# Gated cross-attention and quantised FFN: order of the last batch's softmax, Pool's passes and the context matrix in the attention stage

## The chip, the cores and the metric

One core of one Trainium2 chip runs the kernel as a single launch. The metric is the device time in microseconds (us). The kernel before takes 461.97 us, the median of 3 runs (461.82 to 462.2).

## The reference

Four batches of 1024 tokens of width 256 attend to 154 context rows each, then go through an FFN with fake quantisation. Cut to what matters here:

```python
h = layernorm(x)                                   # per batch, 1024 x 256
Sim = (h @ w1)[:, None] + (ctx @ w2)[None, :] + (h * w3) @ ctx.T + b
hq = softmax(Sim, axis=ctx) @ ctx                  # 1024 x 256
Batt = softmax(max(Sim, axis=ctx), axis=tokens)    # 1024 weights per batch
hc = Batt @ h                                      # one row of 256 per batch
x1 = x + tanh(g0) * (concat[h, hq, h*hq, h*hc] @ W_qv + b_qv)
y = layernorm(x1)
out = x1 + tanh(g1) * ffn(y)                       # 768 hidden, quantised weights and activations
```

`hc` needs the maxima of a whole batch, so `h*hc @ W` is folded into a batch matrix: `h @ (W[0] + hc * W[3])`. That matrix `we` can be made only when all 1024 tokens of the batch have scores.

## The kernel before, in words

The kernel has an attention stage, which makes `x1` and `y` (the first 196 us of the profile), and a quantised FFN stage behind it. The change touches only the attention stage. Its 4096 tokens are cut into N = 16 units of 256 tokens, four to a batch (NP = 4). The work is written as a hand-made software pipeline: each engine has its own loop over slots m = 0, 1, 2, ..., 22, with b = m // 4 and s = m % 4, and in a slot each engine issues, in the order of its own loop, pieces of work for different units. Semaphores alone tie the engines to each other, and each engine executes strictly in the order written. Unit n gets its layernorm and its transpose in slot n, its scores in slot n+1, its attention in slots n+2 and n+3, and its projection, residual and second layernorm from slot n+7 on (LAG = 7). Batches 0 to 2 have their end in a slot in which the next batch is already under way; the last batch (b = 3) has nothing behind it.

What each engine does, with the names that the text uses:

- **TensorE (PE)**, L691 to L727. `project(n)` is 12 matmuls, 24 records in the trace (L576, L578, L582): the third part, L582, multiplies by `we` and in the first unit of a batch waits for it (`we_rdy`, L580). In slots 7, 11 and 15 the first unit of a batch is cut into `project_first` (L601, L603) early in the slot and `project_rest` (L613) at its end, which waits for `we`; the last batch's first unit, unit 12, is not cut: it is `project(12)` in slot 19. `turn_h`, `turn_a`, `turn_y` are transposes, `score(n)` L545, `attend(n)` L564, `turn_w` L676 transposes the FFN's weights. `batch_max(b)` (L641) spreads the batch's minimum over the partitions, `batch_cols(b)` (L648, L649) sums the weighted rows into `hc`. In slot 17 `batch_max(3)`, and in slot 18 `batch_cols(3)`, stand in front of `project`, so all later work of TensorE waits behind them.
- **ScalarE (ACT)**, L942 to L975. `exps(n)` L865, `normed(n)` L874, `turned_*` and `attended(n)` copy out of PSUM, `batch_exp(b)` (L921) makes the 1024 token weights, `row_weigh(b)` (L927) applies half of them, `weight_f(i)` (L932) converts a weight matrix.
- **VectorE (DVE)**, L1328 to L1385. `scored(n)` (L1143), `stats(n)`, `residual(n)` (L1167 to L1178: residual, then mean and deviation), `norm_x1(n)` (L1184, two instructions, makes `yb` out of `xa`), `max_y(n)` (L1224), `attended(n)` (L1159), `batch_max(b)` (L1230, L1232), `batch_shift(b)` (L1236), `summary(b)` (L1240 to L1248, makes `we`), `weight_scales`, `weight_unit`, `weight_values(i)` (L1288), `weight_part` (L1294).
- **GpSimd (POOL)**, L448 to L476. `y_std(n)` (L392) is a tiny power that turns the variance of `residual(n)` into the deviation for which `norm_x1(n)` waits; `row_std` (L388) is the same for the first layernorm. The long passes are `row_weigh(b)` (L418, four instructions), `row_pair(b)` (L425), `row_add(b)` (L431, L433, L435), `bias_x(n)` (L443), `weight_q(i, half)` (L405) and `weight_n(i)` (L411).

The chain from the last score of a batch to its `we` runs: DVE `scored`, DVE `batch_max`, PE `batch_max`, DVE `batch_shift`, ACT `batch_exp`, ACT and POOL `row_weigh`, POOL `row_pair` and `row_add`, PE `batch_cols`, DVE `summary`. For the last batch the order of before spreads it over slots 16 to 18. SyncE's queue loads inputs and stores `x1` and the output; it has no part in the change.

The waits that carry most of the argument are these:

```python
# PE, L645: batch_cols waits for POOL's last addition
pe.wait_ge(hs_rdy, b + 1)
# PE, L579: the matrix of the batch, in its first unit
if s == 0:
    pe.wait_ge(we_rdy, b + 1)
# DVE, L1181: norm_x1 waits for POOL's deviation
dve.wait_ge(rstd2_rdy, n + 1)
```

Of the kernel before, what the change touches and what calls it, by code (L numbers as in the profile page):

```python
# [39 lines left out]
B, S, D = 4, 1024, 256  # L40
# [26 lines left out]
def build(nc, x, ctx, g_xattn, g_ffn, w_sim, b_sim, w_qv, b_qv, w_gate, w_up, w_down, out):  # L67
# [145 lines left out]
    with ExitStack() as stack:  # L213
# [70 lines left out]
        N = B * NP  # L284
        W_AT = [10, 14, 17]
        SCALES_AT = [9, 13, 15]
        VALUES_AT = [12, 16, 18]
        NORMS_AT = [12, 18, 19]
        NF = 2 * NP
        WARM = 24  # L290
        HC = P + D
# [89 lines left out]
        def _(pool):  # L381
# [31 lines left out]
            def row_weigh(b):  # L413

                par = b % 2
                pool.wait_ge(eb_rdy, b + 1)
                for t in range(TB // 2, TB):
                    i_ = pool.tensor_scalar(h[:, par, t, :], h[:, par, t, :], eb[:, t:t + 1], 1.0, ALU.mult, ALU.mult)  # L418
                i_.then_inc(hp_rdy, 1)
# [28 lines left out]
            for m in range(N + LAG):  # L448
                b, s = m // NP, m % NP
                if s == 3 and 4 <= m < N + 4:  # L450
                    for n in range(2):
                        bias_x(m - 5 + n)
                if s == 1 and 1 <= b <= B:
                    row_weigh(b - 1)
                if m == N:
                    for n in range(2):
                        bias_x(m - 4 + n)
                if m == N + 1:
                    row_pair(b - 1)
                    row_add(b - 1)  # L460
                if LAG <= m < L + LAG:
                    y_std(m - LAG)
                if s == 1 and 1 <= b < B:
                    row_pair(b - 1)
                if s == 2 and 1 <= b < B:
                    row_add(b - 1)
                if 1 <= m and m + 3 < N:
                    row_std(m + 3)
                if s == 0 and 4 <= m < N:
                    for n in range(2):  # L470
                        bias_x(m - 4 + n)
                for i in range(3):
                    if m in (SCALES_AT[i] + 1, SCALES_AT[i] + 2):
                        weight_q(i, m - SCALES_AT[i] - 1)
                    if m == NORMS_AT[i]:
                        weight_n(i)  # L476
            y_std_last()

# [27 lines left out]
        def _(pe):  # L506
# [184 lines left out]
            for m in range(N + LAG):  # L691
                b, s = m // NP, m % NP
                late = s == 3 and b < B
                if m == N:
                    score(m - 1)
                if m == N + 1:
                    batch_max(b - 1)
                if m == N + 2:
                    batch_cols(b - 1)
                if LAG <= m and not late:  # L700
                    project(m - LAG, b - 1 if s == 1 and b < B else None)
                if LAG <= m and late:
                    project_first(b - 1)
                if m < N:
                    turn_h(m)
                if s == 3 and b + 1 < B:
                    turn_context(b + 1)
                if 1 <= m < N:
                    score(m - 1)
                if 2 <= m <= N + 1:  # L710
                    turn_a(m - 2)
                if s == 1 and b == 1:
                    batch_max(b - 1)
                if s == 3 and 1 <= b < B:
                    batch_cols(b - 1)
                if 3 <= m <= N + 2:
                    attend(m - 3)
                if LAG < m:
                    turn_y(m - LAG - 1)
                if s == 3 and b + 1 < B:  # L720
                    context_bias(b + 1)
                if LAG <= m and late:
                    project_rest(b - 1)
                if m in W_AT:
                    weight_max(W_AT.index(m))
                for i in TURN_AT.get(m, ()):
                    turn_w(i)  # L727
# [106 lines left out]
        def _(act):  # L834
# [107 lines left out]
            for m in range(N + LAG):  # L942
                b, s = m // NP, m % NP
                if m < N:
                    turned_h(m)
                if s == 3 and b + 1 < B:
                    turned_context(b + 1)
                if s == 1 and 1 < b <= B:
                    batch_exp(b - 1)
                if m == N + 1:  # L950
                    row_weigh(b - 1)
                if NF <= m + 1 < N and s < 3:
                    norm_x(m + 1)
                if 2 <= m <= N + 1:
                    turned_a(m - 2)
                if 1 <= m <= N:
                    exps(m - 1)
                if NF <= m + 1 < N and s == 3:
                    norm_x(m + 1)
                if 3 <= m <= N + 2:  # L960
                    attended(m - 3)
                if 1 <= m <= N:
                    normed(m - 1)
                if s == 1 and b == 1:
                    batch_exp(b - 1)
                if s == 1 and 1 <= b < B:
                    row_weigh(b - 1)
                if LAG < m:
                    turned_y(m - LAG - 1)
                if s == 3 and b + 1 < B:  # L970
                    context_k(b + 1)
                if m in VALUES_AT:
                    weight_f(VALUES_AT.index(m))
                for i in TURN_AT.get(m, ()):
                    turned_w(i)  # L975
# [116 lines left out]
        def _(dve):  # L1092
# [235 lines left out]
            for m in range(N + LAG - 1):  # L1328
                b, s = m // NP, m % NP
                late = s == 3 and b < B  # L1330
                if m == N + 1:
                    batch_shift(b - 1)
                if 4 <= m <= N + 3:
                    attended(m - 4)
                if m == N:
                    scored(m - 1)
                    batch_max(b - 1)
                    normed(m - 1)
                if m == N + 2:
                    summary(b - 1)  # L1340
                if m == 0:
                    norm_x(3)
                if 3 <= m and m + 1 < NF:
# [7 lines left out]
                if s == 0 and LAG < m <= N:  # L1351
                    norm_x1(m - LAG - 1)
                    max_y(m - LAG - 1)
                if LAG <= m and not late:
                    residual(m - LAG)
                if 1 <= m < N:
                    scored(m - 1)
                if s == 0 and 1 <= b < B:
                    batch_max(b - 1)
                if 1 <= m and m + 3 < N:  # L1360
                    if s == 1:
                        dve.wait_ge(xr_in[b], 16)
                    stats(m + 3)
# [3 lines left out]
                    batch_shift(b - 1)  # L1367
                if LAG <= m and not late:
                    norm_x1(m - LAG)
                if s == 3 and 1 <= b < B:  # L1370
                    summary(b - 1)
                if LAG <= m and not late:
                    max_y(m - LAG)
                for i in range(3):
                    if m == SCALES_AT[i]:
                        weight_scales(i)
                    if m == W_AT[i]:
                        weight_unit(i)
                    if m == VALUES_AT[i]:
                        weight_values(i)  # L1380
                if LAG <= m and late:
                    residual(m - LAG)
# [237 lines left out]
```

## Time and profile before

| what | value |
|---|---|
| median of 3 runs | 461.97 us (461.82 to 462.2) |
| the profiled execution's own time | 459.6 us |
| its span in the trace | 457.8 us |
| mean granted TensorE clock | 0.992 of full |
| TensorE matmul, busy | 433.4 us, 95% of the span |
| VectorE, busy | 363.4 us, 79% |
| ScalarE, busy | 274.6 us, 60% |
| GpSimd, busy | 110.7 us, 24% |
| attention stage | the first 196 us of the span |
| FFN stage | from 196 us to the end |

All times of the trace are counted from the start of the span. In a timeline row the columns are: start, length, engine, line and operation, what is written and read, how many such instructions stand in a row, and in brackets how long the engine had been idle before, and which engine and line ended that. Slot borders can be read from TensorE: slot 11 ends with the matmuls of L613 at 86.81, slot 15 with those at 126.15, and slot 18 starts with L648 at 152.54. The profiled execution was 2.4 us quicker than the median of the runs, and its time is 1.8 us above its span.

### The profile page before, as it was taken

The page shows a single profiled execution, that of the slowest core. Times are in us where ns is not written, and L with a number is a line of the kernel's source. Part 1 is how long each engine was busy: PE and PEld are TensorE (multiplying, and loading weights), DVE is VectorE, ACT ScalarE, POOL GpSimd, SP SyncE. Part 2 cuts the span into 40 slices and gives each one's busy share as a digit, 9 for nine tenths or more (in the row PEclk, how much of TensorE's full clock was granted, in tenths as well). Part 3 has the DMA queues.
Part 4 walks back from the last instruction along what each step waited for, and adds up shares of the span by engine and source line. Part 5 has one row for each costly group of instructions (what it writes and reads, how often), then busy time and mean ns, then how long its engine had stood idle before and what let it go on. Part 6 is the DMA issues. An engine that isn't in the chain of part 4 may idle for free.

```text
span 457.8 us, 6771 instructions
## 1 busy us (share of the span) xinstructions
PE 433.4 (95%) x2432; PEld 297.2 (65%) x2432; DVE 363.4 (79%) x652; ACT 274.6 (60%) x346; POOL 110.7 (24%) x109
## 2 busy tenths in 40 slices
PE   4899999999997698999999999999999999999997
PEld 3788898889876586744444444444444444788886
DVE  6786789797777488886433789999998889898874
ACT  2677365556525023284334599999296779987760
POOL 1239274365744453100000013334100000000000
PEclk9999999999999799999999999999999999999999
DMA  7950002000200020110000000000000000344442
GB/s 242 314 166 0 1 2 92 1 0 3 92 1 0 0 94 0 43 50 0 0 0 0 1 1 1 0 0 0 1 0 0 0 0 0 117 139 139 137 137 70
DMA packets 20672, 21.13 MB, mean 46 GB/s; under 512 B 825, under 2 KB 20392, under 8 KB 20648
## 3 DMA queue, kind: packets, MB, share of 16 engines
q1 hardware_dynamic: 20628, 20.82, 14.4%
q8 instruction: 14, 0.23, 0.2%
q14 instruction: 10, 0.08, 0.1%
q10 hardware_dynamic: 20, 0.00, 0.0%
HBM read 12.43 MB, written 8.39 MB: 45 GB/s over the span
## 4 chain that ended last, share of the span: by engine, by line
PE 44%; DVE 24%; issue 19%; ACT 7%; POOL 4%; DMA 1%; ACTq 0%; POOLq 0%; DVEq 0%
PE ps L785 12%; PE ps L750 9%; PE ps L755 5%; DVE cols L1452 4%; DVE yb L1184 4%; PE ps L576 3%; PE ps L578 3%; PE ps L582 3%; DVE hid L1468 2%; ACT hid L1012 2%; PE ps L564 2%; PE ps L545 1%; PE ps L613 1%; POOL h L418 1%; ACT ag L1017 1%
## 5 line engine op out<-in xcount | busy, mean ns | idle before, releaser
L750 PE MATMUL ps<-xh,wuh 128*128 128x512 f16 x192 | 72.8, 379 | 0.8 <-DVE gq L1491 0.8
L750 PE MATMUL ps<-xh,wul 128*128 128x512 f16 x192 | 72.8, 379 | 0.0
L755 PE MATMUL ps<-xl,wuh 128*128 128x512 f16 x192 | 57.2, 379 | 0.0
L1431 DVE TENSOR_REDUCE cols<-hid x10 | 22.9, 2286 | 24.3 <-ACT hid L989 24.3
L785 PE MATMUL ps<-wdl,oh 128*128 128x256 f16 x168 | 37.4, 273 | 0.0
L785 PE MATMUL ps<-wdh,oh 128*128 128x256 f16 x168 | 37.4, 273 | 0.0
L750 PE MATMUL ps<-xh,wgl 128*128 128x512 f16 x96 | 36.4, 379 | 0.0
L750 PE MATMUL ps<-xh,wgh 128*128 128x512 f16 x96 | 36.4, 379 | 0.0
L989 ACT ACTIVATE hid<-ps 128x2048 f32 x10 | 18.8, 1875 | 27.5 <-PE ps L755 27.5
L750 PEld LDWEIGHTS ps<-xh,wuh 128*128 (+1 forms) x192 | 18.8, 98 | 24.0 <-issue 1.8
L482 POOL PARTITION_ALL_REDUCE cols<-cols x4 | 1.5, 374 | 135.0 <-DVE cols L1391 135.0
L755 PEld LDWEIGHTS ps<-xl,wuh 128*128 (+1 forms) x192 | 18.8, 98 | 22.7
L750 PEld LDWEIGHTS ps<-xh,wul 128*128 (+1 forms) x192 | 18.8, 98 | 22.4
L1184 DVE TENSOR_SCALAR yb<-xa,cols 128x256 f32<-128x256 f32 x30 | 23.7, 832 | 11.6 <-POOL cols L392 11.6
L564 PE MATMUL ps<-aT,cx 77*128 77x256 f32 x128 | 30.5, 381 | 0.0
L857 ACT ACTIVATE hT<-ps 128x512 f32<-128x512 f32 x16 | 9.4, 590 | 33.9 <-PE ps L531 33.9
L1491 DVE TENSOR_TENSOR gq<-gq,ps 128x2048 bf16<-128x2048 int16 x11 | 25.1, 2286 | 5.3 <-ACT au L1041 5.3
L1074 ACT ACTIVATE oq<-hid,cols 128x1536 int16 (+1 forms) x15 | 23.6, 1571 | 9.6 <-DVE ol L1547 9.6
L1468 DVE CUSTOM_DVE_ANT_0 hid<-ag,sq 128x2048 f32<-128x2048 int16 x12 | 29.1, 2424 | 0.2
L755 PE MATMUL ps<-xl,wgh 128*128 128x512 f16 x96 | 28.6, 379 | 0.1
L1452 DVE TENSOR_REDUCE cols<-ps 128x1 f32<-128x2048 f32 x12 | 27.4, 2286 | 1.6 <-PE ps L755 1.6
L576 PE MATMUL ps<-wv,hqT 128*128 128x256 f32 x104 | 27.7, 391 | 0.0
(223 smaller groups left out, 1039.8 us busy)
## 6 DMA issues: line engine op xcount, KB each, us to landing
x_scratch<-xa SPq DMA_DIRECT2D x4, 1024.0 KB, 4.4
xo<-x_scratch SPq DMA_DIRECT2D x16, 256.0 KB, 2.7
out_dram<-xo SPq DMA_DIRECT2D x15, 256.0 KB, 2.2
xa<-in_x SPq DMA_DIRECT2D x3, 1024.0 KB, 12.7
xa<-in_x SPq DMA_DIRECT2D x4, 256.0 KB, 4.5
wv<-in_L_xattn_W_qv SPq DMA_DIRECT2D x1, 1024.0 KB, 8.4
wr<-in_L_ffn_w_gate SPq DMA_DIRECT2D x1, 768.0 KB, 10.1
wr<-in_L_ffn_w_up SPq DMA_DIRECT2D x1, 768.0 KB, 11.5
```

The lines of the kernel that those rows point to most:

```text
L564: mm = pe.matmul(hq_bank[:, d * PT:(d + 1) * PT], cx[b][0:JP, k, d * P:(d + 1) * P], aT[0:JP, n % 3, k, :], start=k == 0, stop=k == 1)
L576: pe.matmul(o_, hqT[:, par, d, q], wv[:, KD + d, :], start=d == 0, stop=False)
L750: pe.matmul(ps[hf][:, q, :], w_[:, d, ds(k * P, P)], xh[:, d, n], start=d == 0 and w_ is wh, stop=False)
L755: mm = pe.matmul(ps[hf][:, q, :], wh[:, d, ds(k * P, P)], xl[:, d, n], start=False, stop=d == KD - 1)
L785: mm = pe.matmul(down_ps(par)[:, t], o_[:, par, k, q], w_[:, k, :], start=not low and k == 0 and w_ is wdh, stop=low and k == KF - 1)
L989: act.activation(unit(hid, k, hf), ps_half(hf), ACT.Copy).then_inc(half_free[hf], 1)
L1074: act.activation(oq[:, par], hid[:, :, ds(c * CD, CD)], ACT.Copy, scale=c_co).then_inc(oqa_rdy, 1)
L1184: i_ = dve.tensor_scalar(yb[:, n % 2, t, :], xa[:, 2 * n + t, :], mv2[:, t, 0:1], rstd2[:, t:t + 1], ALU.subtract, ALU.mult)
L1431: dve.tensor_reduce(gmx[:, ds(k * 2 + hf, 1)], unit(hid, k, hf), AX.X, ALU.max, apply_absolute_value=True).then_inc(gm_done, 1)
L1452: dve.tensor_reduce(umx[:, u:u + 1], ps_half(u % 2), AX.X, ALU.max, apply_absolute_value=True).then_inc(half_free[u % 2], 1)
L1468: dve.tensor_tensor_reduce(half_of(hid, u), ag[:, u % 2, :], sq[u % 2][:], 1.0, 0.0, ALU.mult, ALU.max, pmx[:, u:u + 1]).then_inc(p_rdy, 1)
L1491: dve.tensor_tensor(g_.bitcast(BF16), g_, ps_half(hf), ALU.mult).then_inc(half_free[hf], 1)
```

## The change

It moves work within the slots of the four hand-written orders; no instruction is added or removed.

- POOL: `bias_x` of slots 8 and 12 (and 4) moves from the end of the slot to its head, in front of `y_std` and `row_std`. `row_pair(b-1)` follows `row_weigh(b-1)` directly, in front of `y_std`. For the last batch both move from slot 17 to slot 16, and `row_add(3)` stays in slot 17, in front of `y_std(10)`. `weight_n(1)` moves in slot 18 in front of `y_std(11)`; `weight_n(2)` moves from the end of slot 19 to slot 20 in front of `y_std(13)`.
- PE: `batch_max(3)` moves from the head of slot 17 into slot 16 behind `turn_a(14)`; `batch_cols(3)` stays in slot 18 but moves behind `project(11)`.
- ACT: in slot 16 `exps(15)` goes ahead of `turned_a(14)`, and `batch_exp(3)` and `row_weigh(3)` come from slot 17 into slot 16.
- DVE: `batch_shift(3)` comes from the head of slot 17 into slot 16, with `normed(15)` directly ahead of it, both behind `norm_x1(8)` and `max_y(8)` and in front of `residual(9)`. `summary(3)` stays in slot 18 and moves behind `residual(11)`. `weight_values(2)` moves in slot 18 from the end to in front of `residual(11)`. `summary(1)` and `summary(2)`, in slots 11 and 15, move in front of `stats` and `normed`.

```diff
-        NORMS_AT = [12, 18, 19]
+        NORMS_AT = [12, 18, 20]
...
# POOL
-                if s == 1 and 1 <= b <= B:
-                    row_weigh(b - 1)
-                if m == N:
+                if s == 0 and 4 <= m < N + 4:
                     for n in range(2):
                         bias_x(m - 4 + n)
+                if s == 1 and 1 <= b < B or m == N:
+                    row_weigh(b - 1)
+                    row_pair(b - 1)
                 if m == N + 1:
-                    row_pair(b - 1)
                     row_add(b - 1)
+                for i in range(3):
+                    if m == NORMS_AT[i] and i > 0:
+                        weight_n(i)
                 if LAG <= m < L + LAG:
                     y_std(m - LAG)
-                if s == 1 and 1 <= b < B:
-                    row_pair(b - 1)
...
-                if s == 0 and 4 <= m < N:
-                    for n in range(2):
-                        bias_x(m - 4 + n)
...
-                    if m == NORMS_AT[i]:
+                    if m == NORMS_AT[i] and i == 0:
                         weight_n(i)
# PE
-                if m == N + 1:
-                    batch_max(b - 1)
-                if m == N + 2:
-                    batch_cols(b - 1)
...
-                if s == 1 and b == 1:
+                if s == 1 and b == 1 or m == N:
                     batch_max(b - 1)
+                if m == N + 2:
+                    batch_cols(b - 1)
# ACT
-                if s == 1 and 1 < b <= B:
+                if s == 1 and 1 < b < B:
                     batch_exp(b - 1)
-                if m == N + 1:
-                    row_weigh(b - 1)
+                if m == N:
+                    exps(m - 1)
...
-                if 1 <= m <= N:
+                if m == N:
+                    batch_exp(b - 1)
+                if 1 <= m < N:
                     exps(m - 1)
...
-                if s == 1 and 1 <= b < B:
+                if s == 1 and 1 <= b < B or m == N:
                     row_weigh(b - 1)
# DVE
-                if m == N + 1:
-                    batch_shift(b - 1)
...
-                    normed(m - 1)
-                if m == N + 2:
-                    summary(b - 1)
+                if m == VALUES_AT[2]:
+                    weight_values(2)
...
+                if m == N:
+                    normed(m - 1)
+                    batch_shift(b - 1)
                 if LAG <= m and not late:
                     residual(m - LAG)
+                if m == N + 2:
+                    summary(b - 1)
...
+                if s == 3 and 2 <= b < B:
+                    summary(b - 1)
...
-                if s == 3 and 1 <= b < B:
+                if s == 3 and b == 1:
                     summary(b - 1)
...
-                    if m == VALUES_AT[i]:
+                    if m == VALUES_AT[i] and i < 2:
                         weight_values(i)
```

## Rows read from the trace of the kernel before

**Rows 1.** The page: busy time, share of the span, instructions of each engine.

```profile
PE 433.4 (95%) x2432; PEld 297.2 (65%) x2432; DVE 363.4 (79%) x652; ACT 274.6 (60%) x346; POOL 110.7 (24%) x109
```

**Rows 2.** Busy time by stretch, the second half of the attention stage (then clock, DMA).

```profile
126.00:196.00 70.00, 60.63 (x309) 51.16 (x310) 52.20 (x115) 19.06 (x39) 27.57 (x26) 0.95 0.09 30
```

**Rows 3.** Timeline of TensorE, slots 11, 15 and 18 to 21.

```profile
85.98 0.76 PE L522 MATMUL ps<-cxT,w2b 128*128 128x154 f32 x4 [0.98 <-DVE cols L1242]
86.81 1.99 PE L613 MATMUL ps<-we,hT 128*128 128x256 f32 x8
...
126.15 2.00 PE L613 MATMUL ps<-we,hT 128*128 128x256 f32 x8 [0.86 <-DVE we L1248]
...
152.54 1.01 PE L648 MATMUL ps<-ones,h 128*128 128x1 f32 x4 [6.49 <-POOL h L435]
...
153.84 2.05 PE L576 MATMUL ps<-wv,hqT 128*128 128x256 f32 x4
...
160.68 1.89 PE L564 MATMUL ps<-aT,cx 77*128 77x256 f32 x8
...
162.84 1.03 PE L576 MATMUL ps<-wv,hqT 128*128 128x256 f32 x4
...
168.02 0.60 PE L621 MATMUL ps<-ident,yb 128*128 128x128 f32 x4
...
176.36 0.66 PE L621 MATMUL ps<-ident,yb 128*128 128x128 f32 x4 [1.25 <-DVE yb L1184]
...
179.43 1.03 PE L576 MATMUL ps<-wv,hqT 128*128 128x256 f32 x4
```

**Rows 4.** Busy time by microsecond around the stall; the third column from the right is PEclk.

```profile
150.00:151.00 1.00, 0.00 (x0) 0.00 (x0) 0.00 (x0) 0.00 (x0) 0.92 (x2) 0.60 0.00 0
...
156.00:157.00 1.00, 1.00 (x4) 0.73 (x4) 0.88 (x5) 0.00 (x0) 0.00 (x0) 0.50 0.00 0
157.00:158.00 1.00, 1.00 (x6) 0.90 (x5) 0.93 (x4) 0.00 (x0) 0.00 (x0) 0.98 0.00 0
```

**Rows 5.** Timeline of GpSimd, slots 17 to 19.

```profile
145.95 1.84 POOL L418 TENSOR_SCALAR h<-h,cols 128x256 f32<-128x256 f32 x4 [3.96 <-ACT cols L921]
...
151.76 0.72 POOL L435 TENSOR_TENSOR h<-h 128x256 f32<-128x256 f32 x1
...
153.11 1.48 POOL L405 TENSOR_TENSOR wr<-wr,wri 128x768 f32<-128x768 f32 x1
...
163.63 2.77 POOL L411 TENSOR_TENSOR wr<-wr,wsc 128x1536 f32<-128x1536 f32 x1
166.37 2.60 POOL L443 TENSOR_TENSOR xa<-xa,txb 128x512 f32<-128x512 f32 x2
```

**Rows 6.** Timeline of VectorE in slot 18: the two instructions of norm_x1(11), one by one.

```profile
163.71 2.85 DVE L1184 TENSOR_SCALAR yb<-xa,cols 128x256 f32<-128x256 f32 x1 [0.81 <-POOL cols L392]
...
166.48 1.35 DVE L1184 TENSOR_SCALAR yb<-xa,cols 128x256 f32<-128x256 f32 x1
```

**Rows 7.** Timeline of VectorE, slots 15 to 19.

```profile
125.22 0.88 DVE L1248 SCALAR_TENSOR_TENSOR we<-wv,cols 128x256 f32<-128x256 f32 x2
...
132.09 1.38 DVE L1232 TENSOR_SCALAR diag<-ident,cols 128x128 f32<-128x128 f32 x1
...
140.57 1.88 DVE L1184 TENSOR_SCALAR yb<-xa,cols 128x256 f32<-128x256 f32 x2 [0.81 <-POOL cols L392]
...
153.18 1.88 DVE L1184 TENSOR_SCALAR yb<-xa,cols 128x256 f32<-128x256 f32 x2 [6.28 <-POOL cols L392]
...
157.81 0.88 DVE L1248 SCALAR_TENSOR_TENSOR we<-wv,cols 128x256 f32<-128x256 f32 x2
...
173.13 3.18 DVE L1184 TENSOR_SCALAR yb<-xa,cols 128x256 f32<-128x256 f32 x2 [0.81 <-POOL cols L392]
```

**Rows 8.** Timeline of ScalarE in slot 17: the last batch's exponentials.

```profile
145.47 0.28 ACT L921 ACTIVATE cols<-cols 128x8 f32<-128x8 f32 x1
```

**Rows 9.** Timeline of GpSimd and of TensorE in slots 4 to 6.

```profile
28.59 2.78 POOL L443 TENSOR_TENSOR xa<-xa,txb 128x512 f32<-128x512 f32 x2
...
34.12 0.66 PE L554 MATMUL ps<-ident,sc 128*77 128x128 f32 x4 [0.68 <-ACT sc L874]
```

## The prediction

> **What bounds the kernel now.** I read the page first: TensorE is busy for 95% of the span [rows 1], so a gain can only be idle or slow time of TensorE. Busy time by stretch says where that is: of the 70 us from 126 to 196 us TensorE works 60.6, at a mean clock of 0.95 [rows 2]. Next I read TensorE's timeline there, for its gaps and for who ended each [rows 3]. The largest is 6.49 us in front of 152.54: `batch_cols(3)` waits for Pool's last addition (151.76 + 0.72 [rows 5]), and `project(11)` stands behind it. The clock falls during this gap: it is 0.60 in the microsecond from 150 to 151, stays at 0.50 (1.2 of 2.4 GHz) until 157, and is back after it [rows 4]. So `project(11)` took 6.84 us (153.84 to 160.68) where `project(12)` took 5.18 (162.84 to 168.02) [rows 3], 1.66 lost. `batch_cols` took 1.30 (152.54 to 153.84); if half of that is the clock, 0.65 is lost too. Stall and clock together: 6.49 + 1.66 + 0.65 = 8.8 us. Smaller gaps are 0.98 in slot 11, 0.86 in slot 15 and 1.25 in front of 176.36 [rows 3].
>
> Then I read the chain behind the large gap. Batch_exp(3) runs at 145.47 [rows 8], since it is in slot 17 behind `weight_f(1)`; Pool weighs the rows from 145.95 on and ends at 152.48 [rows 5]. Vector waits 6.28 us for `y_std(10)` behind that same Pool work, until 153.18 [rows 7].
>
> **Slots 11 and 15.** `summary` goes ahead of `stats` (slot 11) and of `normed` (slot 15). In slot 11 it saves the 1.15 us of `stats`; the matmuls at 86.81 can start when `we` is there, at about 85.7, and the 0.98 wait of the row before goes too: 1.1 us. In slot 15 `normed` waits for exponentials and holds `summary` back; ahead of it, `we` is ready at 124.95 in place of 126.1 (its end by 125.22 + 0.88 [rows 7]), and TensorE starts the matmuls of 126.15 at about 125.2: 1.0 us. What `stats` and `normed` give up, 1.3 us, is covered, as their users come a slot later.
>
> **Slots 16 and 17**, on the clock of before (slot 11's gain taken off at the end). TensorE runs `score(15)`, `project(9)` and `turn_a(14)` until 133.7, `batch_max(3)` until 133.9, `attend(13)` until 135.6. Vector: `diag` is held by `weight_q` until 132.4. Now `bias_x(12)` and (13), 1.25 each (2.60 for two [rows 5]), hold the two halves of `norm_x1(8)` until 133.7 and 134.95; `max_y(8)`, `normed(15)`, `batch_shift(3)` end at 136.1. Batch_exp(3) ends at 136.6, before at 145.9 [rows 8]: 9.3 sooner. Pool's `row_weigh` (1.84 [rows 5]) and `row_pair` (1.3) end at 139.8, `y_std(9)` at 140.5, `weight_q` (1.48 [rows 5]) at 142.0, the three additions of `row_add(3)` (3.3, and 0.8 for a Vector instruction let in between) at 146.1. TensorE reaches `batch_cols(3)` at 149.3, behind `project(10)` and `project(11)`. So **the stall of 6.49 and the half clock behind it are gone**, with 3 us to spare. Every moved instruction of POOL is in this; none issues a DMA, and SyncE's queue isn't touched.
>
> **What is late next.** Vector. Norm_x1(9) has to wait until 140.5 for `y_std(9)`, which now stands behind `row_weigh` and `row_pair`, and is then held by `weight_q` and the first addition until 143.4. `max_y`, `weight_values(1)`, `attended(13)` and `residual(10)` follow: 148.7. Then y_std(10) at 149.45, `weight_q` (1.48) until 150.95 and, directly behind, `weight_n(1)` (2.77) until 153.75 [rows 5]: the two halves of `norm_x1(10)` end at 151.1 and 153.9. TensorE has finished `attend(15)` at 151.5 and wants that `yb`: **first new wait, 2.4 us**. Vector goes on with `max_y`, `weight_unit(2)`, `attended(14)`, `weight_values(2)`, 3.3 us, to 157.2; `residual(11)`, 1.9, to 159.1; `summary(3)`, 1.26 (0.15 + 0.22 + 0.88 [rows 7]), to 160.35. The diff puts the last two in this order. Before, `we` was there at 158.7 (157.81 + 0.88 [rows 7]), long ahead of its use. Now `project(12)` starts at 154.4 and at 156.1 wants `we`: **second new wait, 4.2 us**. It resumes at 160.35 and ends at 163.8, before at 168.02 [rows 3].
>
> After that: norm_x1(11) is held by `bias_x(14)` and (15) only, not by `weight_n(1)`: 2.1 us in place of 4.13. `weight_n(2)` is still the next pass of Pool after `y_std(12)`, with nothing between; here the diff changes nothing, and norm_x1(12) keeps its 3.18 us [rows 7]. Its `yb` is there at 169.95 and TensorE wants it at 170.8, so the 1.25 goes. Turning the weights in slot 20 waits about 0.4 for Vector's `weight_part`. `project(14)` starts at 172.9, before at 179.43 [rows 3]: 6.5 us sooner. Check by waits: pure work between 125.2 and `project(14)` is 40.7 us, so of before's 53.3 us from 126.15, 12.6 were waits and half clock; now they are 2.4 + 4.2 + 0.4 = 7.0. 12.6 - 7.0 + 1.0 (slot 15) = 6.6, the same within 0.1. From 180 us on nothing changes its order, and the FFN stage needs only the last unit: the gain is kept whole.
>
> **Slots 4 to 13.** In slot 4 the two `bias_x` leave 28.59, where they held a Vector layernorm for 2 us and so TensorE for 0.68 at 34.12 [rows 9] and 0.44 before. At 23.3 they hold `attended(0)` and norm_x(5) instead; `normed(3)` comes 1.4 later and TensorE waits 1.05 for `turn_a(3)`. I get 1.05 lost and 1.25 won, 0.2 us gained; bounds are 1.0 lost (nothing comes back) and 1.2 gained. In slots 8 to 13 the moved passes run where Pool was idle, and `row_pair` ahead of `y_std` changes 1.3 us of blocking into 1.3 us of waiting: nothing, as TensorE has work queued for over 2 us there; if that cover is gone, 0.6 per slot.
>
> **The sum.** 6.5 (slots 15 to 21) + 1.1 (slot 11) + 0.2 = 7.8 us: 459.6 becomes 451.8 for the profiled execution. The median of the runs is 2.4 us above it, so 461.97 becomes 454.2.
>
> **The rivals.**
> - *Vector is less late than worked out* (0.17). The new waits are 7 us because Pool's passes catch `norm_x1(10)` twice. If its second half gets in ahead of `weight_n(1)`, the first wait goes and the second shrinks to about 3. Against: [rows 6]. Gain 9.5 to 11, 451 to 452.5.
> - *A queue of Pool passes keeps Vector out until it is empty* (0.07). Then norm_x1(9) also waits for all three additions, 2.3 us more down to `summary(3)`: gain 5.5, 456.5. Against: two separate ends in [rows 6]. The Trainium skill, "SBUF — State Buffer", section "SBUF: two separate sides", says that whichever of the two engines starts first holds the shared ports "for the whole instruction" while the other "fully blocks"; it doesn't say who wins at the border, and by its strictest reading this rival holds.
> - *The clock falls in the new waits* (0.18). Before, it fell within the idle stretch of 6.49 us [rows 3, 4]; the second new wait is two thirds as long, with only 2 us of work between it and the first. Half clock behind it costs about what it cost before, 2.3: gain 5.5, 456.5. For: the waits stand close together. Against: no shorter wait here (up to 1.25 us) moved the clock. The Trainium skill, "TensorE: Matmul & The Clock Gate", Part 1, says that the array drops to half clock when idle and regains full clock only by sustained activity; this speaks against the change, for it makes one long wait into two nearer ones.
> - *Slower* (0.04). The same clock, but it stays down: after the first new wait TensorE's work never runs long enough to bring it back before the next wait. From 7.8 us of work run at half rate on, the change loses: between 154 us and the end of the stage TensorE has some 35 us of work. If 12 us of it run at half rate, 466. Against: before, 4.7 us after work had resumed the clock was back [rows 4].
> - *No change* (0.02): another wait of the same length takes the place of 152.54, which would need `hs_rdy` at 155, 9 us later than I get.
> - The rest, 0.52, is the forecast, with a range of its own of 452.7 to 455.5.
>
> **How the numbers follow.** Range 451.0 to 457.8: it takes in the first three rivals and the bounds of slot 4, and leaves out a combination of losses. A measurement of this kernel can tell about 0.2% (0.9 us) from no change. Faster 0.93, same 0.03, slower 0.04.
>
> **What would show it.** Right: no gap over 0.5 us in front of L648; batch_exp(3) near 135.5 on the new clock; `project(12)` with a gap in front of its first L582 of 3 to 4 us, ended by DVE L1248; a gap near 2 us in front of `turn_y(10)`; PEclk 1.00 around it; `project(14)` near 171.6. Wrong: a gap in front of L648 still ended by POOL L435, an L582 without a wait, a clock of 0.5 near 158, or FFN rows whose lengths differ from before.

## The result, and the profile after

The changed kernel takes 456.42 us, the median of 4 runs (454.66 to 457.08), against 462.09 for the kernel before. One of the 4 runs of before took 760.31 us, far from the other three (461.82 to 462.20), and only those three count in the ratio. The ratio is 0.9883 with a 95% interval of 0.9836 to 0.9930: faster, by 1.2%, which is 5.4 us (5.7 by the two medians). Two more sets of runs gave 0.9882 (0.9852 to 0.9912) and 0.9872 (0.9850 to 0.9895). The forecast was 454.2 with a range of 451.0 to 457.8, so the time lies inside the range, but 2.2 us above the number, where two of the rivals stood (456.5: the clock falls in the new waits, or a queue of Pool passes keeps Vector out); the traces decide between them below. The profiled execution took 455.91 us, where 451.8 was forecast for it; it is 3.7 us under the profiled one of before (459.6), which was a quick one of its kind.

TensorE's timeline after, slots 11, 15 and 18 to 22; a project(n) begins with L574 here, where it was L576 before (answers to [rows 3]):

```profile
85.00 0.77 PE L520 MATMUL ps<-cxT,w2b 128*128 128x154 f32 x4 [0.17 <-DVE cols L1240]
85.82 1.99 PE L611 MATMUL ps<-we,hT 128*128 128x256 f32 x8
...
124.34 1.99 PE L611 MATMUL ps<-we,hT 128*128 128x256 f32 x8
...
148.46 0.50 PE L646 MATMUL ps<-ones,h 128*128 128x1 f32 x4
...
152.80 0.66 PE L619 MATMUL ps<-ident,yb 128*128 128x128 f32 x4 [1.78 <-DVE yb L1182]
...
160.25 2.07 PE L580 MATMUL ps<-we,hT 128*128 128x256 f32 x4 [5.06 <-DVE we L1246]
...
166.03 0.60 PE L619 MATMUL ps<-ident,yb 128*128 128x128 f32 x4
...
175.37 1.03 PE L574 MATMUL ps<-wv,hqT 128*128 128x256 f32 x4
```

The stall of 6.49 us in front of `batch_cols(3)` is gone: L646 starts at 148.46 with nothing to wait for. In its place stand the two waits that were forecast: 1.78 us for the `yb` of norm_x1(10), and 5.06 us for the batch matrix in the middle of `project(12)`. The 16 matmul records behind the second took 5.78 us (160.25 to 166.03) where 3.45 is their time at full clock (164.57 to 168.02 in the trace of before). The clock says why (answers to [rows 4]; the third column from the right is PEclk):

```profile
154.00:156.00 2.00, 1.19 (x6) 0.71 (x4) 1.93 (x6) 0.09 (x1) 0.00 (x0) 1.00 0.00 0
156.00:158.00 2.00, 0.00 (x0) 0.00 (x0) 1.89 (x7) 1.48 (x1) 0.00 (x0) 0.99 0.19 68
158.00:160.00 2.00, 0.00 (x0) 0.00 (x0) 1.94 (x3) 0.00 (x0) 2.00 (x3) 0.50 1.02 347
160.00:163.00 3.00, 2.75 (x7) 2.21 (x8) 2.97 (x5) 0.00 (x0) 1.32 (x1) 0.50 0.25 82
```

It falls near 158, inside the second wait, is at 0.61 in the microsecond from 164 and at full behind it. That is a loss of 5.78 - 3.45 = 2.33 us.

The other side of the waits is Vector, which from 146 to 162 us has hardly a gap left. Its timeline after (answers to [rows 6, 7]) and Pool's (answers to [rows 5]):

```profile
148.41 4.34 DVE L1182 TENSOR_SCALAR yb<-xa,cols 128x256 f32<-128x256 f32 x2 [0.81 <-POOL cols L392]
...
155.91 0.75 DVE L1165 SCALAR_TENSOR_TENSOR xa<-ps,cols,xa 128x512 f32<-128x512 f32 x1
...
157.83 0.16 DVE L1238 RECIPROCAL cols<-ps 128x1 f32<-128x1 f32 x1
158.03 0.22 DVE L1240 TENSOR_SCALAR cols<-ps,cols 128x2 f32<-128x2 f32 x1
158.28 1.91 DVE L1246 SCALAR_TENSOR_TENSOR we<-wv,cols 128x256 f32<-128x256 f32 x2
160.12 1.67 DVE L1182 TENSOR_SCALAR yb<-xa,cols 128x256 f32<-128x256 f32 x2
```

```profile
148.34 1.48 POOL L405 TENSOR_TENSOR wr<-wr,wri 128x768 f32<-128x768 f32 x1
149.78 2.82 POOL L411 TENSOR_TENSOR wr<-wr,wsc 128x1536 f32<-128x1536 f32 x1
158.00 0.69 POOL L392 TENSOR_TENSOR cols<-cols 128x2 f32<-128x2 f32 x1 [5.41 <-DVE cols L1176]
158.66 2.67 POOL L443 TENSOR_TENSOR xa<-xa,txb 128x512 f32<-128x512 f32 x2
```

Norm_x1(10) takes 4.34 us for 0.7 us of work: `weight_q` and `weight_n(1)` run back to back on Pool in front of it. And the last two instructions of `summary(3)`, 0.88 us before [rows 7], take 1.91: `bias_x` starts at 158.66, directly behind `y_std(11)`, and holds the second of them.

### The profile page after: what moved, and what is told of

Its sections match the earlier page's. It is cut to its first block, busy times and chain, and to the rows that moved or that the text cites. A ratio compares the mean times of both kernels' runs of the same rounds, so it can differ in the third digit from the quotient of the medians.

```text
span 454.1 us, 6771 instructions
## 1 busy us (share of the span) xinstructions
PE 433.1 (95%) x2432; PEld 297.5 (66%) x2432; DVE 363.0 (80%) x652; ACT 275.0 (61%) x346; POOL 110.9 (24%) x109
## 4 chain that ended last, share of the span: by engine, by line
PE 42%; DVE 26%; issue 20%; ACT 6%; POOL 4%; DMA 1%; ACTq 0%; POOLq 0%; DVEq 0%
PE ps L781 12%; PE ps L746 9%; PE ps L751 5%; DVE cols L1454 4%; DVE yb L1182 4%; PE ps L580 3%; PE ps L574 2%; PE ps L576 2%; DVE hid L1470 2%; ACT hid L1010 2%; PE ps L543 2%; PE ps L562 2%; POOL h L418 1%; ACT ag L1015 1%; DVE st L1169 1%
## 5 line engine op out<-in xcount | busy, mean ns | idle before, releaser
L580 PE MATMUL ps<-we,hT 128*128 128x256 f32 x104 | 27.7, 390 | 5.1 <-DVE we L1246 5.1
L1182 DVE TENSOR_SCALAR yb<-xa,cols 128x256 f32<-128x256 f32 x30 | 24.7, 865 | 8.6 <-POOL cols L392 8.6
```

The source lines that it names most:

```text
L580: mm = pe.matmul(o_, hT[:, par, d, q], we[:, par, d, :], start=False, stop=d == KD - 1)
L1182: i_ = dve.tensor_scalar(yb[:, n % 2, t, :], xa[:, 2 * n + t, :], mv2[:, t, 0:1], rstd2[:, t:t + 1], ALU.subtract, ALU.mult)
```

## The experiments

The base of each comparison is the kernel before, run on the same chip beside it. Line numbers of the versions differ by a few from those of the changed kernel. Where a gain over the changed kernel is given, its median on the same chip is taken: 455.66 us for experiments 2, 3 (the first version) and 4, and 455.84 for the others. The traces don't all start alike: over the profiles of experiments 1 to 6 `batch_cols(3)` begins between 148.27 and 149.26 us, so a difference of times under 1 us between two of them says little unless that start is the same.

**1. The changed kernel again**, as a base, in two sets.

> The changed kernel once more, as the base of the other three. Theory A (the changed kernel loses 5.1 us in project(12)'s wait for the batch matrix and 2.4 us to the half clock behind it; Vector's order makes the wait): 456 us, 5.5 to 6.5 us under the kernel before, a wait of 5 us in front of the first L580 of project(12), the clock at half from about 158 to 164 us. Theory B (the moment of the clock's fall is chance): runs of the same kernel differ by 1 to 3 us, and a profile with the clock at full behind the wait turns up.

> The changed kernel again, as the base for the three others on the same chip: 456 us, 1.2% under the kernel before.

Measured 455.66 us in the first set and 455.84 in the second. What theory B asked for turned up in part: single runs of the kernel lie between 454.6 and 457.4, and the clock in the first set's profile behaves otherwise than in the one above:

```profile
153.00:154.00 1.00, 1.00 (x6) 0.88 (x5) 0.90 (x5) 0.56 (x1) 0.00 (x0) 0.58 0.00 0
154.00:155.00 1.00, 1.00 (x4) 0.77 (x3) 0.97 (x4) 0.04 (x1) 0.00 (x0) 0.50 0.00 0
...
156.00:157.00 1.00, 0.77 (x2) 0.10 (x1) 0.97 (x3) 1.00 (x1) 0.00 (x0) 0.71 0.00 0
157.00:158.00 1.00, 0.00 (x0) 0.00 (x0) 0.90 (x7) 0.40 (x1) 0.11 (x1) 1.00 0.51 173
...
160.00:161.00 1.00, 0.86 (x2) 0.77 (x3) 1.00 (x2) 0.00 (x0) 1.00 (x1) 0.50 0.58 190
```

Here it falls behind the first wait already, is full again at 157, and is at half once more when the second wait ends; `project(12)` ends at 165.29. The profile of the second set is like the one above (5.07 us of wait, `project(12)` ends at 165.86). So the moment of the fall differs between executions of one kernel, but all three pay behind the second wait. A profile with the clock at full there did not turn up.

**2. Summary(3) in front of residual(11).** It asks whether the place of the wait matters, or only Vector's total lateness.

```diff
-                if LAG <= m and not late:
-                    residual(m - LAG)
                 if m == N + 2:
                     summary(b - 1)
+                if LAG <= m and not late:
+                    residual(m - LAG)
```

> The changed kernel with summary(3) in front of residual(11) instead of behind it in slot 18. Theory A: summary follows weight_values(2) at 155.9 us and isn't held by bias_x, so the matrix is there at 157.2 in place of 160.2; the second wait falls from 5.1 to 2 us and the clock stays at full; but then turn_y(11) waits some 2 us for a norm_x1(11) that comes behind it, and project(14) starts 2.5 us sooner than in the changed kernel: 453.5 us. Theory C (the wait is only where Vector's lateness shows; its place does not matter): project(14) starts at the same time as in the changed kernel, 456 us, with the wait in front of turn_y(11).

Measured 453.50 us, ratio 0.9835 (0.9803 to 0.9867). TensorE's and Vector's timelines of this version:

```profile
157.50 1.58 PE L580 MATMUL ps<-we,hT 128*128 128x256 f32 x4 [2.11 <-DVE we L1246]
...
162.86 0.66 PE L619 MATMUL ps<-ident,yb 128*128 128x128 f32 x4
```

```profile
156.56 0.88 DVE L1246 SCALAR_TENSOR_TENSOR we<-wv,cols 128x256 f32<-128x256 f32 x2
...
160.18 2.62 DVE L1182 TENSOR_SCALAR yb<-xa,cols 128x256 f32<-128x256 f32 x2 [0.81 <-POOL cols L392]
```

The matrix takes 0.88 us, not 1.91, and the wait is 2.11. Theory A's time came out, partly by luck; its working did not in one part: the clock fell here too, after 158, and the half rate hid the wait that was foreseen in front of turn_y(11), as its `yb` comes at 162.8 anyway. Theory C, 456 us, falls.

**3. TensorE kept busy in the wait**: 20 matmuls whose results nobody reads.

```diff
                     if s == 0:
+                        if b == B - 1:
+                            for i in range(20):
+                                pe.matmul(hT_bank[:, 0:P], ones[:], ident[:], start=True, stop=True)
                         pe.wait_ge(we_rdy, b + 1)
```

> The changed kernel with 20 matmuls of 128x128 (float32, results unused) into a free bank between the second and the third part of project(12), in front of its wait for the batch matrix: some 4.4 us of work in a wait of 5.1. Theory A: the wait keeps its end (160.2 us), the clock stays at full, project(12) ends 2.3 us sooner (163.7 in place of 166.0) and all behind it too: 453.7 us. Theory C (Vector would be late anyway, so the clock costs nothing): project(12) is shorter but residual(12) starts no sooner, 456 us.

Measured 458.62 us, slower than the changed kernel, through a flaw of the edit: it stands in a loop over both halves of `project(12)`, so a second 20 (4.4 us) ran behind the wait. Against the kernel before the ratio is 0.9939 (0.9920 to 0.9958). With these 4.4 us taken off it would be some 454, but that is arithmetic, no measurement. The same with `and t == 0`:

> The changed kernel with the 20 matmuls once, between the second and third part of the first half of project(12) (in r_warm they stood in both halves, and the second 20 lay on the path: 4.4 us). Theory A: the wait for the batch matrix still ends at 160.2 us, the clock is at full there, project(12) is through 2.0 to 2.3 us sooner than with half clock behind the wait, and since Vector's residual(12) waits for it all behind comes sooner: 453.7 us against 455.7. Theory C (Vector would be late anyway): 455.7 us, no gain.

Measured 454.59 us, ratio 0.9844 (0.9812 to 0.9877) against 0.9882 and 0.9872 for the changed kernel; the intervals overlap, so this alone decides nothing. In its profile the clock had fallen already behind the first wait, the 20 matmuls ran at half rate for part of their way and ended at 161.05, 0.9 us after the matrix was there. So both waits were filled, with 7 and 18 matmuls:

> The changed kernel with 7 such matmuls (1.5 us) in the wait of turn_y(10) and 18 (4.0 us) in the wait for the batch matrix, since the clock was seen to fall in the first wait already. Theory A: the clock stays at full all through, project(12) ends at 163.6 us in place of 165.3 to 166, and the time is 1.7 to 2.3 us under the changed kernel, with less spread between runs. Theory C (Vector would be late anyway): the same time as the changed kernel.

Measured 453.55 us (453.21 to 454.13 in 5 runs), ratio 0.9814 (0.9798 to 0.9829) against 0.9872 (0.9850 to 0.9895) for the changed kernel beside it. Its clock and TensorE's timeline (L583 is the third part of project(12), L622 turn_y(11)):

```profile
158.00:160.00 2.00, 1.18 (x11) 0.98 (x9) 1.97 (x3) 0.00 (x0) 2.00 (x3) 1.00 1.04 346
160.00:162.00 2.00, 1.77 (x8) 1.59 (x9) 1.97 (x4) 0.00 (x0) 1.29 (x1) 1.00 0.33 109
```

```profile
160.23 1.13 PE L583 MATMUL ps<-we,hT 128*128 128x256 f32 x4 [1.05 <-DVE we L1252]
...
163.78 0.60 PE L622 MATMUL ps<-ident,yb 128*128 128x128 f32 x4
```

The matrix comes no sooner (160.2 us, as in the changed kernel; `batch_cols(3)` begins at 148.44 here and at 148.46 there), the clock is at full, and project(12) is through at 163.78 in place of 166.03 (165.29 and 165.86 in the other two profiles): 2.25 us. The medians differ by 2.3. So **the half clock behind the new wait costs the changed kernel 2.3 us**, and nothing else covers it; theory C falls. The runs spread over 0.9 us (5 runs) where those of the changed kernel beside them spread over 1.9 (4 runs). That the clock makes the whole of that difference isn't shown: the slowest of the 4, 457.4 us, has the highest mean clock of them, 0.993.

**4. Weight_n(1) back behind y_std(11).** It tests the rule for Pool's passes by itself.

```diff
                 for i in range(3):
-                    if m == NORMS_AT[i] and i > 0:
+                    if m == NORMS_AT[i] and i > 1:
                         weight_n(i)
...
-                    if m == NORMS_AT[i] and i == 0:
+                    if m == NORMS_AT[i] and i < 2:
                         weight_n(i)
```

> The changed kernel with weight_n(1) back behind y_std(11), at the end of slot 18. Theory A (a Vector instruction waits out each Pool pass under way, one gets in at each border): norm_x1(10) takes 1.9 us in place of 4.3, the 1.8 us wait of turn_y(10) goes, Vector reaches summary(3) 2.4 us sooner, but now weight_n(1) holds its second half until 159: the matrix is there at about 159.2, one wait of 6.2 us in place of 1.8 and 5.1, the clock falls: 455.3 us. Theory D (where a pass stands does not matter as long as it is off TensorE's path): same time as the changed kernel, 456.2 us, within 0.5.

Measured 455.15 us, ratio 0.9864 (0.9831 to 0.9896). By the time alone theories A (455.3) and D (within 0.5 of 456.2) can't be told apart, and against the changed kernel's 455.66 nothing is gained clear of the spread; by the trace they can. Vector and Pool of this version:

```profile
148.55 1.88 DVE L1182 TENSOR_SCALAR yb<-xa,cols 128x256 f32<-128x256 f32 x2 [0.82 <-POOL cols L392]
...
155.97 3.42 DVE L1246 SCALAR_TENSOR_TENSOR we<-wv,cols 128x256 f32<-128x256 f32 x2
```

```profile
156.34 2.77 POOL L411 TENSOR_TENSOR wr<-wr,wsc 128x1536 f32<-128x1536 f32 x1
159.07 2.71 POOL L443 TENSOR_TENSOR xa<-xa,txb 128x512 f32<-128x512 f32 x2
```

Norm_x1(10) takes 1.88 us, as worked out, and the second half of the matrix waits out `weight_n(1)` until 159.4 (expected 159.2). TensorE has one wait of 6.12 us in front of 159.45 (expected 6.2). The place of the pass decides which Vector instruction it falls on: `weight_n(1)` holds `norm_x1(10)` in the changed kernel and `summary(3)` here. That the time stays nearly the same is no sign that the place doesn't matter: one wait went (1.78 us), the other grew (5.06 to 6.12), and more of TensorE's time behind it passes at half clock (6.0 us, until about 165.4, in place of 4.5, until about 164.8).

**5. Pool waits for norm_x1 before its next pass.**

```diff
                 pool.tensor_tensor(rstd2, vp2, mhalf[:, 0:2], ALU.pow).then_inc(rstd2_rdy, 1)
+                if 9 <= n <= 12:
+                    pool.wait_ge(y_rdy, n + 1)
```

> The changed kernel in which Pool, behind y_std(9) to y_std(12), waits until norm_x1 of the same unit is done before it starts its next long pass. Theory A (what makes Vector late is that a pass of Pool starts in front of norm_x1 each time): norm_x1(9), (10), (12) take 0.7 us each in place of 2.8, 4.3 and 3.2, the passes fall on weight_values and attended instead, the matrix is there at 156.4 in place of 160.2, the wait of turn_y(10) is gone: 449.5 us with the clock at full, 451 to 451.5 with it at half behind the wait. Theory F (the passes only move on to the next Vector instruction, nothing is won): 455.5 us.

Measured 451.84 us, ratio 0.9773 (0.9744 to 0.9802). Vector and TensorE of this version (L1184 is norm_x1(10), L582 the third part of project(12)):

```profile
147.75 0.73 DVE L1184 TENSOR_SCALAR yb<-xa,cols 128x256 f32<-128x256 f32 x2 [0.82 <-POOL cols L392]
```

```profile
157.41 2.08 PE L582 MATMUL ps<-we,hT 128*128 128x256 f32 x4 [3.77 <-DVE we L1248]
```

Norm_x1(9) to (12) now take 0.73 us each; the matrix ends a wait of 3.77 us at 157.41 (expected 156.4), and the clock is at half behind it, the case given as 451 to 451.5. Theory F falls. The passes fall on `weight_values` and `attended` instead: `attended(14)`, 0.69 us in the changed kernel, takes 3.15.

**6. The same, with summary(3) at the head of slot 18.**

```diff
+                if m == N + 2:
+                    summary(b - 1)
                 if 4 <= m <= N + 3:
                     attended(m - 4)
...
-                if m == N + 2:
-                    summary(b - 1)
```

> As r_wait_y, and summary(3) at the head of Vector's slot 18, in front of attended(14). Theory A: the matrix is there at 152.5, ahead of its use at 153, no wait of TensorE over 1 us is left and the clock stays at full: project(14) starts at 166 in place of 175, 447 us. Theory C (Vector's total work sets the end, the order of it does not matter): the same as r_wait_y.

**Measured 447.31 us (446.04 to 447.57), ratio 0.9674 (0.9649 to 0.9698)**: 8.5 us under the changed kernel, 14.8 under the kernel before. Its clock is 1.00 all through in the profile (0.999 to 1.000 on the mean of each run), and one wait is left behind slot 16:

```profile
150.98 2.82 DVE L1248 SCALAR_TENSOR_TENSOR we<-wv,cols 128x256 f32<-128x256 f32 x2
...
158.01 0.73 DVE L1184 TENSOR_SCALAR yb<-xa,cols 128x256 f32<-128x256 f32 x2 [0.81 <-POOL cols L392]
```

```profile
153.85 1.13 PE L582 MATMUL ps<-we,hT 128*128 128x256 f32 x4
...
158.80 0.66 PE L621 MATMUL ps<-ident,yb 128*128 128x128 f32 x4 [1.23 <-DVE yb L1184]
```

The matrix is still held by a pass (2.82 us for 0.88), but it is ready at 153.8, when TensorE asks for it. It was expected at 152.5, and project(14) at 166 where it starts at 167.53; this trace runs 0.8 to 0.9 us later than the changed kernel's from its first slots on, so 0.5 to 0.7 us of each is a miss of the working. Is it then the early summary alone? The same place of `summary(3)` without Pool's waits:

> The changed kernel with summary(3) at the head of Vector's slot 18, in front of attended(14), but without Pool's waits. Theory A (Vector's chain of norm_x1 behind Pool's passes sets the pace as soon as the matrix is early): the matrix is there at 155.7, the wait for it is 0.7 us, but turn_y(11) waits 2 to 4 us for norm_x1(11), and the time is that of the version with summary ahead of residual, 453.5 us (0.4 to 0.6% under the changed kernel). Theory H (the place of summary is all that matters): as r_best, 447.3 us.

Measured 453.28 us, ratio 0.9810 (0.9793 to 0.9828): as theory A had it. TensorE waits no more for the matrix (0.7 was expected; the clock is at half from about 153.3 to 156.7, and the slower matmuls fill that time), but 2.32 us for norm_x1(11):

```profile
162.82 0.66 PE L619 MATMUL ps<-ident,yb 128*128 128x128 f32 x4 [2.32 <-DVE yb L1182]
```

By the medians the summary alone is worth 2.6 us, Pool's waits alone about 4, both together 8.5. Each alone leaves TensorE a long wait (2.32 and 3.77 us) with half clock behind it in its profile; only both together leave neither.

**7. The parts of the change.** The kernel before with summary(1) and (2) moved ahead of stats and normed, nothing else:

```diff
+                if s == 3 and 2 <= b < B:
+                    summary(b - 1)
                 if 1 <= m and m + 3 < N:
...
-                if s == 3 and 1 <= b < B:
+                if s == 3 and b == 1:
                     summary(b - 1)
```

> The kernel before with one part of the change alone: summary(1) ahead of stats in slot 11 and summary(2) ahead of normed in slot 15. Theory A: 1.1 us in slot 11 and 1.0 in slot 15, kept through the stall in front of batch_cols(3), whose chain of Vector, ScalarE and Pool is itself driven by TensorE: 2.1 us under the kernel before. Theory E (the stall has its own clock: its chain isn't moved by these two slots): the stall grows by 2.1 us and nothing is gained.

Measured 459.43 us, ratio 0.9941 (0.9922 to 0.9961), so 2.7 us (1.8 to 3.6), where 2.1 was expected. The stall stays what it was and only starts sooner:

```profile
150.67 1.01 PE L648 MATMUL ps<-ones,h 128*128 128x1 f32 x4 [6.48 <-POOL h L435]
```

Before it ended at 152.54 [rows 3]: 1.9 us are kept through it, and theory E falls. This profile shows a second fall of the clock, which the profile of before hasn't: to 0.54 in the microsecond from 176, behind the two short waits in front of turn_y(13) and of the turning of the weights. Both versions have these two waits, 1.25 and 0.75 us long:

```profile
174.71 0.66 PE L621 MATMUL ps<-ident,yb 128*128 128x128 f32 x4 [1.25 <-DVE yb L1184]
176.12 2.79 PE L676 MATMUL ps<-ident,wr 128*128 128x128 f32 x12 [0.75 <-DVE wgl L1294]
178.70 1.43 PE L576 MATMUL ps<-wv,hqT 128*128 128x256 f32 x4
```

From turn_y(13) to the second part of project(14) it is 5.26 us here (174.71 to 179.97), and 3.94 in the profile of before (176.36 to 180.30): the second fall costs 1.3. The reverse, the changed kernel without everything in slots 4 to 15, its edit being the diff's first POOL and the `summary` hunks undone:

> The changed kernel without its parts in slots 4 to 15: bias_x of slots 4, 8 and 12 and row_pair of batches 0 to 2 where they were before, summary(1) and summary(2) back behind stats and normed. What is left is the last batch's part. Theory A: the two summaries are worth 2.1 us, Pool's passes in slots 4 to 13 about 0.2: 458.2 us, 2.3 over the changed kernel and some 3.5 under the kernel before. Theory G (Pool's passes in slots 4 to 13 are worth something of their own): over 3 us slower than the changed kernel.

Measured 457.82 us, ratio 0.9902 (0.9885 to 0.9919): 2.0 us over the changed kernel beside it, 4.4 under the kernel before. The two summaries account for these 2.0 within the error, so these runs show no gain from Pool's passes in slots 4 to 13.

## Why the prediction was right, and where it was off

- **The stall**: right. Batch_exp(3) was forecast at about 135.5 and runs at 135.30; L646 has no wait. That the stall's half clock (1.66 + 0.65) goes with it was right as well.
- **Slots 11 and 15**: 1.1 + 1.0 + 0.2 (slot 4) forecast; TensorE's slot 15 ends with matmuls at 124.34, before at 126.15 [rows 3]: 1.8 of the 2.3. In slot 4 TensorE waits 0.82 for turn_a(3), where 1.05 was forecast, and `batch_cols(0)` comes 0.17 us sooner.
- **What is late next**: right in kind and place. Norm_x1(9) was put at 2.9 us (140.5 to 143.4) and takes 2.83, norm_x1(10) at 4.4 (149.5 to 153.9) and takes 4.34, norm_x1(12) keeps its 3.17. First new wait: 2.4 forecast, 1.78 measured.
- **The term that was mis-sized: "summary(3), 1.26 (0.15 + 0.22 + 0.88)".** It took 2.36 us (157.83 to 160.19), since L1246 reads and writes SBUF alone and falls under the very rule that the prediction had set up; it had been applied to four operations and not to this one. It let `bias_x` hold only `norm_x1(11)`. `y_std(11)` needs `residual(11)` alone, so Pool was free to start `bias_x` while `summary` ran. 1.0 us; the second wait became 5.06 us in place of 4.2.
- **The step that failed: full clock behind the new waits.** It was a rival at 0.18, priced at 2.3; filling the waits with work gave back 2.3. The argument against it, that no shorter wait (up to 1.25 us) had moved the clock, rested on one execution and did not hold: in experiment 7 the clock fell behind this very wait of 1.25 us and one of 0.75. The Trainium skill, "TensorE: Matmul & The Clock Gate", Part 1, has the array drop to half clock in idleness; these traces agree (0.50 from 158 us on, inside the wait of 5.06). It says too that the moment at which the full clock comes back varies from run to run: in the three profiles of the changed kernel that is at about 163.4, 164.5 and 164.8 us (worked out from the clock of each microsecond).
- **The rival that a queue of Pool passes keeps Vector out falls**, though its number, 456.5, came as near as the clock's. By it norm_x1(9) would have waited for all three additions; it was through at 142.51, and the last addition ended at 145.12:

```profile
139.68 2.83 DVE L1182 TENSOR_SCALAR yb<-xa,cols 128x256 f32<-128x256 f32 x2 [2.48 <-POOL cols L392]
```

```profile
143.79 1.33 POOL L435 TENSOR_TENSOR h<-h 128x256 f32<-128x256 f32 x1
```

The Trainium skill, "SBUF — State Buffer", section "SBUF: two separate sides", leaves open who wins at the border between passes; the 4.34, 1.91 and 3.42 us above all fit one Vector instruction at each border.
- **The sum**: project(14) was forecast at about 171.6 and came at 175.37, 3.8 us late: 1.0 for `summary`, 2.3 for the clock, 0.5 left over. Forecast gain 7.8 less 3.8 is 4.0; TensorE is 4.06 ahead at that point (179.43 before [rows 3]), and the profiled executions differ by 3.7 at the end.
- **The number was helped by luck.** The forecast for the profiled execution, 451.8, was missed by 4.1 us; that of the median by 2.2 only, since the prediction added 2.4 us for the distance from the profiled execution to the median, and for the changed kernel that distance is 0.5. The mean clock of each run hints at where the 2.4 come from. In the 17 runs of before beside experiments 1, 2 and 4, the 5 with a mean clock of 0.992 or more took 458.6 to 460.0 us, the 12 below it 461.2 to 462.7; the profiled execution of before had 0.992. Over the three sets of experiments 5 of 39 runs of before have 0.992 or more; of the changed kernel, with the runs of the result, 8 of 14 have it. That fits the second fall of the clock seen in experiment 7: the change takes away the wait of 1.25 us that the fall stands behind. No profile of the kernel before itself with a second fall was taken, so that remains an inference.
- **A reading that was off**: against the rival *slower* the prediction has the clock back 4.7 us after work resumed; by [rows 3, 4] it is 4.5.

## What to carry to other kernels

When a long wait of the busiest engine is removed, work out what that engine asks for next and who makes it: here a wait of 6.5 us became two of 1.8 and 5.1. The cure for both was to put the one result needed (the batch matrix) ahead of work that nobody was waiting for, and to hold Pool's long passes back until Vector had its short one done. Where a long pass of Pool holds Vector, as here (0.73 us of norm_x1 became up to 4.34), its place is a choice of whom it holds: start it right behind the short instruction that matters, with a wait if need be, not right in front of it. And price a new wait of TensorE with the half clock behind it, not by its length alone; one profile in which a short wait left the clock alone is no proof that it always will.

## What the runs showed of the hardware

- TensorE's clock fell behind the wait of 1.8 us in front of turn_y(10) in five of the eight profiles that have it (in that of experiment 1 to 0.50 in the microsecond from 154), and in the three others only in or behind the wait for the matrix that follows. In experiment 7 it fell behind waits of 1.25 and 0.75 us; in the profile of before it did not behind the same two. With both waits filled it was 1.00 throughout.
- Letting Vector in between two Pool passes costs Pool too: with Pool's waits the first addition took 1.99 us where it took 1.30 in the changed kernel, with `weight_values` and `attended` let in around it. The row is that of experiment 6, whose L433 is L431 of the changed kernel; in experiment 5 it took 1.99 as well.

```profile
142.77 1.99 POOL L433 TENSOR_TENSOR h<-h 128x512 f32<-128x512 f32 x1
```
